# A macaron block on one core: token preparation moved out of the first rounds of each batch, into eight short turns of its second round

## The reference, cut to what matters

```python
x = x + 0.5 * ffn(layernorm(x))     # 8 experts, threshold routing with capacity
x = x + attn(layernorm(x))          # 16 heads of width 16, 4 "nodes" per head
x = x + 0.5 * ffn(layernorm(x))

# attn, per batch b and head h
q, k, v = x @ Wq, x @ Wk, x @ Wv;  probs = softmax(x @ Wr)       # 4 nodes
pos = cumsum(probs over tokens) - probs                            # soft position
cos_w, sin_w = sum over nodes of probs * (cos, sin)(pos * freq), interpolated
q_r, k_r = rotate(q), rotate(k) by cos_w, sin_w
scores = q_r @ k_r.T / sqrt(16) + log(probs @ probs.T + 1e-8)     # causal
out = softmax(scores) @ v;  return out @ Wo
```

## Time and profile before

| | us |
|---|---|
| median of 3 runs | 2910.24 (2907.36 to 2912.67) |
| the profiled execution: its time | 2896.46 |
| its span, first to last instruction | 2894.6 |
| units of the attention (first to last exp) | 536.0 to 2528.7 |
| busy PE / DVE / ACT / POOL | 2448.1 / 1711.7 / 1702.9 / 997.9 |

### The profile page before, as it was taken

How to read it: one execution, slowest core, us unless ns; L and a number is a source line. 1 busy time by engine, 2 the same in 40 slices (tenths; PEclk the granted TensorE clock), 3 DMA queues, 4 the chain that set the end, 5 groups by cost and what they waited for, 6 DMA issues and landing times. The chain is left out here.

```text
span 2894.6 us, 104325 instructions
## 1 busy us (share of the span) xinstructions
PE 2448.1 (85%) x45990; PEld 1896.7 (66%) x45990; DVE 1711.7 (59%) x3627; ACT 1702.9 (59%) x2174; POOL 997.9 (34%) x1497
## 2 busy tenths in 40 slices
PE   7298444587899999899999989999999999973885
PEld 4165222466788887778888777888877888841553
DVE  7732278788576567866566786666676111167431
ACT  6222123456677777667777766777776777662221
POOL 1188700334222224423222442222244222110787
PEclk9699776799999999999999999999999999986997
DMA  6555401221212112212111221211122111162565
GB/s 233 160 103 101 78 18 30 60 53 47 60 57 56 48 46 79 66 49 59 55 53 52 79 66 53 58 53 53 54 74 69 44 47 49 42 204 72 105 102 74
DMA packets 185109, 207.28 MB, mean 72 GB/s; under 512 B 35984, under 2 KB 151712, under 8 KB 184480
## 3 DMA queue, kind: packets, MB, share of 16 engines
q1 hardware_dynamic: 158880, 165.60, 19.3%
q0 software_dynamic: 24576, 34.10, 7.6%
q10 hardware_dynamic: 1152, 0.26, 0.0%
HBM read 131.68 MB, written 76.02 MB: 72 GB/s over the span
## 5 line engine op out<-in xcount | busy, mean ns | idle before, releaser
L1697 PEld LDWEIGHTS at_mix<-at_val,at_ew 128*64 128x64 f32 x34816 | 1223.7, 138 | 241.3 <-issue 36.0
L1281 ACT ACTIVATE at_ew<-at_ring 128x1024 f32<-128x1024 f32 (+1 forms) x1280 | 1124.7, 898 | 364.4 <-PE at_ring L1679 358.2
L1697 PE MATMUL at_mix<-at_val,at_ew 128*64 128x68 f32 x34816 | 1263.0, 224 | 44.7 <-DVE at_mixed L1543 28.7
L1679 PE MATMUL at_ring<-at_qT,at_kT 98*64 98x512 bf16 (+3 forms) x5120 | 698.9, 353 | 57.9 <-ACT at_ew L1281 35.8
L1202 POOL TENSOR_SCALAR_AFFINE_SELECT at_ew<-at_ew 128x256 f32<-128x256 f32 x512 | 294.3, 579 | 1074.2 <-ACT at_ew L1281 1073.5
L1543 DVE TENSOR_TENSOR at_mixed<-at_mix,at_prob 128x272 f32<-128x272 f32 x256 | 112.3, 439 | 440.4 <-PE at_mix L1697 439.1
L1679 PEld LDWEIGHTS at_ring<-at_qT,at_kT 98*64 98x64 bf16 x5120 | 228.5, 112 | 111.4 <-ACT at_ew L1281 47.6
L1224 POOL TENSOR_TENSOR at_val<-at_vo,at_val 128x256 f32<-128x256 f32 x384 | 267.4, 717 | 7.5
L344 POOL DMA_INDIRECT out_dram<-ffn_xn,ffn_idx_all x128 | 210.0, 1641 | 43.4 <-issue 35.0
L334 POOL DMA_INDIRECT ffn_xn<-table,ffn_idx_all x128 | 126.2, 986 | 278.4 <-DMA ffn_idx_all<-ffn_idx_hi 240.3
L1762 PE MATMUL at_side<-at_w_all,at_turned 128*64 128x512 f32 (+1 forms) x1024 | 197.8, 531 | 13.8 <-DVE at_bounded L1536 5.2
(11 more groups left out here) (243 smaller groups left out, 2727.1 us busy)
## 6 DMA issues: line engine op xcount, KB each, us to landing
table<-ffn_xn SPq DMA_DIRECT2D x32, 512.0 KB, 6.3
q_parts<-at_parts SPq DMA_DIRECT2D x64, 192.0 KB, 2.5
k_parts<-at_parts SPq DMA_DIRECT2D x64, 192.0 KB, 3.0
at_qT<-q_parts SPq DMA_DIRECT2D x128, 96.0 KB
at_kT<-k_parts SPq DMA_DIRECT2D x64, 192.0 KB
ffn_front<-in_L_attn_x_dram SPq DMA_DIRECT2D x16, 512.0 KB, 5.3
ffn_w_in<-in_L_ffn_w_dram SPq DMA_DIRECT2D x32, 256.0 KB, 3.6
at_xin<-out_dram SPq DMA_DIRECT2D x32, 256.0 KB, 6.0
```

Source lines behind the costliest of these rows:

```text
L1281: act.activation(ew[u % NE_BUF][:, a:b], ring[u % 2][:, a:b], ACT.Exp).then_inc(s["exp_ready"], 1)
L1679: lastm = pe.matmul(ring[u % 2][h:h + HALF, at:at + (CH - t) * P], kT[q][:, kc + j * P + h:kc + j * P + h + HALF], qT[q][:, qc + t * P:qc ...
L1697: m = pe.matmul(mix[block_of[u] % 2][h:h + HALF, t * K * VW:(t + 1) * K * VW], ew[u % NE_BUF][:, col + h:col + h + HALF], val[q][:, tile0 ...
```

## The change

1. **Turns follow the rounds.** Round 0 keeps four SHORT turns. The second round of each batch has eight MID turns of 28 units. The first rounds of batches 1 to 3 are BARE: no step of preparation or output in them. Each pair is still ready in time, since the eight MID turns of a batch prepare the eight pairs of the next. In the last second round nothing is left to prepare, and all eight turns carry a `post`.
2. **New places.** MID: PE (1, 3, 6, 8, 10, 12, 14, 17, 21, 23); ACT copy_turned 3, copy_v_logits 5, copy_outputs 8, softmax_exp 7, square 10, high_part 14, middle_part 16, low_part 20, trig 18, copy_qk 25, next_rsqrt 17. PE's weighting without reserve is at places 16 to 22. SHORT on ACT: trig 17 (was 16), low_part 19 (18), next_rsqrt 16 (20).
3. **Small steps on DVE.** Rotation, positions, angles, products and sums are cut in more steps, each at a place of its own; in MID turns products and sums go in quarters.
4. **Rotated tiles in transpose mode.** turn_rotated does eight transposes of 128x128 instead of sixteen matmul calls.

```diff
-    turns, at = [], 0
-    while at < U:
-        m = len(turns)
-        turns.append((at, SHORT if m < N_SHORT else LONG))
-        at += turns[-1][1]
+    rounds = [first_unit[v] for v in range(V) if v == 0 or visits[v][1] != visits[v - 1][1]] + [U]
+    turns, m = [], 0
+    for r in range(len(rounds) - 1):
+        size = rounds[r + 1] - rounds[r]
+        count, kind = (N_SHORT, SHORT) if r == 0 else (N_MID, MID) if r % 2 else (1, BARE)
+        for n in range(count):
+            turns.append((rounds[r] + n * (size // count), size // count, kind, None if kind == BARE else m))
+            m += kind != BARE
...
+    STORE_AT = (20, 21, None)
...
-        BURST = 26
+        BURST, BURST_END = 16, 22
...
-                    if at == (10 if short else 14) and new is not None:
+                    if at == (10, 12, None)[kind] and new is not None:
                         add_up(new)
...
-                SHORT_AT = (3, 6, None, 8, 9, 12, 15, 18, 16, 23, 20)
-                LONG_AT = (4, 6, 10, 8, 16, 18, 20, 23, BURST + 2, BURST + 4, BURST + 3)
+                SHORT_AT = (3, 6, None, 8, 9, 12, 15, 19, 17, 23, 16)
+                MID_AT = (3, 5, 8, 7, 10, 14, 16, 20, 18, 25, 17)
...
-                SHORT_AT = (0, 1, 6, 8, None, 10, 12, 13, 14, 18, 19, 20, 21, 23)
-                LONG_AT = (1, 2, 5, 8, 10, 14, 17, 20, 22, 30, 32, 25, 34, 33)
...
+                AT = {"weights": (1, 1), "rotate": (2, 2), "rotate_2": (2, 3), "join": (3, 4), "squares": (14, 16), "bound": (20, 22),
+                      "residual": (None, 9), "shift": (6, 5), "softmax": (8, 8), "positions": (10, 11), "whole": (10, 11),
+                      "first_angles": (11, 12), "count_turns": (12, 13), "angles": (13, 13), "absolute": (13, 14),
+                      "statistics": (15, 15), "normalise": (23, 18)}
+                PRODUCTS_AT = ({18: 0, 21: 2}, {19: 0, 21: 1, 23: 2, 25: 3})
+                SUMS_AT = ({19: 0, 22: 2}, {20: 0, 22: 1, 24: 2, 26: 3})
...
                             for n in range(4):
                                 for g in range(G):
-                                    for h in range(0, P, HALF):
-                                        at = (g * 4 + n) * P + h
-                                        lastm = pe.matmul(side[h:h + HALF, n * GP + g * P:n * GP + (g + 1) * P],
-                                                          qkr[:, at:at + HALF], ident[:, :],
-                                                          start=(n % 2 == 0 and g == 0), stop=False, skip_group_check=True)
+                                    at = (g * 4 + n) * P
+                                    lastm = pe.matmul(side[:, n * GP + g * P:n * GP + (g + 1) * P], qkr[:, at:at + P], ident[:, :],
+                                                      is_transpose=True, start=(n % 2 == 0 and g == 0), stop=False, skip_group_check=True)
...
-                LONG_AT = (1, 3, 7, 9, 13, 15, 17, 20, 24, BURST)
+                MID_AT = (1, 3, 6, 8, 10, 12, 14, 17, 21, 23)
...
-                    if not short and (at == 0 or at >= BURST):
+                    if kind == MID and BURST <= at <= BURST_END:
                         weigh_until(u)
```

More of the change, by code:

```diff
@@ L825, in build_attention @@
     LEAD = 5
-    SHORT, LONG = 24, 40
-    N_SHORT = 4
+    SHORT, MID, BARE = 0, 1, 2
+    N_SHORT, N_MID = 4, 8
     TAIL = TP - 4
@@ L926, in fin_of @@
     def fin_of(m):
-        return LEAD + m - 1 if LEAD + m - 1 < TP else None
+        return LEAD + m - 1 if m is not None and LEAD + m - 1 < TP else None
     with ExitStack() as ctx:
@@ L1060, in schedule @@
             first_visit()
-            for m, (start, size) in enumerate(turns):
-                for at in range(min(size, U - start)):
-                    unit(start + at, at, size == SHORT, new_of(m), fin_of(m), posts.get(m))
+            for start, size, kind, m in turns:
+                for at in range(size):
+                    unit(start + at, at, kind, new_of(m), fin_of(m), posts.get(m))
             last_projections()
@@ L1132, in first_visit, with unit @@
                     load_heads(1)
-                def unit(u, at, short, new, fin, post):
+                def unit(u, at, kind, new, fin, post):
                     if u + 2 in first_unit and u + 2 < U:
@@ L1641, in unit @@
[L1641 to L1650, removed]
+                    if kind == BARE:
+                        return
@@ new lines, in unit @@
+                    step = [name for name in AT if AT[name][kind] == at]
+                    per = 2 if kind == SHORT else 1
+                    if fin is not None:
+                        if "weights" in step:
+                            turn_weights()
+                        if "rotate" in step:
+                            rotate(fin, 0)
+                        if "rotate_2" in step:
+                            rotate(fin, 1)
+                        if "join" in step:
+                            join_halves()
+                        if "squares" in step:
+                            largest_squares(fin)
+                        if "bound" in step:
+                            bound(fin)
@@ new lines, in unit @@
+                    if post is not None and "residual" in step:
+                        add_residual(post, 0, 1)
+                    if new is not None:
+                        if "shift" in step:
+                            shift_logits(new)
+                        if "softmax" in step:
+                            node_softmax(new)
+                        if "positions" in step:
+                            positions(new)
+                        if "whole" in step:
+                            whole_positions()
+                        if "first_angles" in step:
+                            first_angles(new)
+                        if "count_turns" in step:
+                            count_turns()
+                        if "angles" in step:
+                            angles()
+                        if "absolute" in step:
+                            absolute_angles(new)
+                        if at in SUMS_AT[kind] and at in PRODUCTS_AT[kind]:
+                            node_sums(SUMS_AT[kind][at], per)
+                            node_products(new, PRODUCTS_AT[kind][at], per)
+                        elif at in PRODUCTS_AT[kind]:
+                            node_products(new, PRODUCTS_AT[kind][at], per)
+                        elif at in SUMS_AT[kind]:
+                            node_sums(SUMS_AT[kind][at], per)
@@ L1652, in last_projections @@
+                    if more:
+                        if "statistics" in step:
+                            statistics(new + 1)
+                        if "normalise" in step:
+                            normalise(new + 1)
                 def last_projections():
```

88 lines of the change are left out of this document (41 added, 47 removed).

## The result

| | before | after |
|---|---|---|
| median, us | 2910.61 | 3090.10 (3088.8 to 3097.3) |
| ratio, 95% interval | | 1.0623 (1.0604 to 1.0642) |
| the profiled execution: time / span | 2896.46 / 2894.6 | 3088.8 / 3086.8 |
| units of the attention | 1993 | 2176 |

The change makes the kernel 6.2% slower. The forecast was 3070 us, 5.5% slower. The windows of the changed kernel by round: length, busy PE, PEld, DVE, ACT, POOL, granted clock, DMA share, GB/s.

The account below looks back on a forecast made before the run. PE was taken to bound the second rounds, without idle. From 2896.5: - 50.7 - 18 + 214 + 3 + 12 = 3056.8, plus 13.8 to the median gives 3070 us, 5.5% slower; range 2945 to 3125, the forecast's own 3020 to 3110.

Parts of the forecast that it names:

- To which sort of turn MID belongs: MID turns in second rounds: PE waits 9.3 us each, near SHORT's 9.5, where LONG has none; 214 us over 23 turns.
- First rounds, laid bare: First rounds of batches 1 to 3: PE's waits for late mixing and masks all go, 50.7 us saved.
- Transposes: turn_rotated on PE: eight transposes take 1.3 us instead of 1.91 per pair, 18 us saved in all.
- ACT's copies: MID turns: PE waits for ACT's steps two places behind its own, 3.1 us per turn together.
- The sine step: ACT's sines in MID turns: 4.2 us of PE wait plus 0.6 at low_part, 4.8 per turn; bounds 1.6 and 4.8.
- The 0.6 for low_part: MID turns, place 20: low_part finds no reserve after the sines, so PE waits 0.6 us more.
- The clock: MID turns: lower clock level after the sines' wait costs PE 1.4 us per turn; bounds 0 and 2.5.
- PE's busy time: Sign in second rounds: a MID turn with post near 56 us, 46 to 47 of them PE busy.
- Round 0: SHORT turns: next_rsqrt ahead of the sines waits for statistics, 3 us per turn, 12 in all; bounds 0 and 20.
- The rival by which MID behaves like LONG: Second rounds: added waits are hidden, 2854 us, or 2880 with half the bare rounds' gain; chance 0.13.
- The head loads: Rival in bare rounds: loads late by 2 us in each of 24 visits, 48 us lost, 3118 us; 0.07 with another rival.

Follow-up runs that it names:

- e4: Changed kernel with e2's next_rsqrt places, plus ACT's MID copies three places behind PE's steps instead of two; ratio 1.0107 to the kernel before.
- e5: Changed kernel with MID places laid out as LONG's, sines under PE's project_qk, SHORT places as before; ratio 0.9736 to the kernel before.
- e6: e5 with five of ACT's MID steps one place earlier, two places behind PE instead of three; ratio 0.9927 to the kernel before.
- e1: Kernel before with only the rotated tiles turned in transpose mode; 2878.12 against 2896.14 us, ratio 0.9939.
- e2: Changed kernel with next_rsqrt behind the sines on ACT (MID 19, SHORT 20, other ACT SHORT places as before); ratio 1.0369 to the kernel before.
- e3: Changed kernel with sine and cosine of pairs 9 to 31 replaced by two scaled copies, no table loads; 2978.96 us, ratio 1.0286 to the kernel before.
- e7: e5 with the sine step alone moved from place 26 to 21 of ACT's MID turn; ratio 1.0170 to the kernel before.

## Why the prediction was right, point by point

- **To which sort of turn MID belongs.** Right, and shown: by the waits in the trace of after, by e4 (three places for two), e5 and e6.
- **First rounds, laid bare.** Forecast was that all 50.7 us of idle go. They went down to 2.0 to 2.4 us per round, 6.6 in all, and in e5 to 10. The reason given was right: in the first round of batch 1 PE waited 10.3 us for DVE's mixing and 4.3 us for POOL's masks, and in the changed kernel it waits for neither. e5 against e1 gives 59 us, more than the forecast, but only 41 of them are idle time; the 18 us of busy time, which went together with the lower level of the clock, were not forecast.
- **Transposes.** Forecast 18 us, measured 18 (e1), with some luck: the saving was taken as 0.6 us per pair and it is 0.8 by the records' lengths, and a part of it did not reach the time. The Trainium skill's 275 ns for one ("TensorE: Matmul & The Clock Gate", Part 4) agrees with the trace, where a record lasts 279 ns on average. Paid one behind the other they would have made the kernel slower, and that is not what this case shows: eight take 1.09 us.
- **ACT's copies.** Forecast 0.4, 0.1, 0.2, 1.0, 0.6, 0.8. In the turn shown: 0.26, none over 0.12 for the next two, 0.88, 0.65, 0.81. Their sum is 2.7 instead of 3.1 us of idle.
- **The sine step.** Forecast 4.2 us of wait, of which next_rsqrt's standing for the statistics was named; measured 0.88 + 3.58 = 4.5, and ACT's standing 1.89. e2 shows the part of the statistics, e3 that of the tables, e7 that the step alone does it. The last pair has no statistics behind it to wait for, and there the changed kernel's own wait is 2.33 us, as in e2. The 0.6 for low_part did not come in the changed kernel; in e2, where the long wait is shorter, 0.50 stands there.
- **The clock.** Forecast 1.4 us per turn, and right. A turn with a post that has 0.97 is 1.2 us longer than one that has 1.00, and one that has 0.94 is 2.1 to 2.5 us longer. Behind the wait of 3.58 us, which 22 turns have, the clock stayed up in 4, fell for the shorter time in 12 and for the longer in 6, which makes about 1.3 us on average.
- **PE's busy time.** This is the term that the sum did not have. A turn of 57.2 us has 49.95 us of PE busy time, and even one with the clock at 1.00 has 48.56, where e5 has 47.00 for the same work; the prediction said 46 to 47 of 56. So 1.4 us are the lower level, and 1.6 us are there at full clock: this is the step that fell short, since a stop costs PE more than its idle time. The sum per turn was 9.3 us instead of 57.2 - 47.0 = 10.2.
- **Round 0.** Forecast + 12 besides the transposes, found + 16 with them. Against e1's 199.8 us, which has the transposes too, it is + 18, so this term was a third too small. ACT stands 6.04 us for the statistics in a SHORT turn (PE 5.66 us, then 2.23), and e2 gives back 14 us by ACT's list alone. The wait for the head load at the end of the round went from 6.46 to 5.48 us.
- **The whole.** The forecast is 20 us under the measured median, but a part of that is chance. Its sum was reckoned between profiled executions and comes to + 160 us; between the two profiled executions the difference is 192, so that 32 us are missing. The three dense rounds take 1347 us where e5 takes 1114, 233 more against 216 forecast (17 of the 32). Round 0 adds 6, the stretch behind the attention 9, and the transposes gave 4 us less over the units than was put down for them; the bare rounds gave 9 more, which takes away from it. The rest is in the last round, the lead and rounding. The medians are closer, because the profiled execution of the kernel before was 14 us under its median and the changed kernel's only 1.
- **Not forecast.** Behind the last exp the changed kernel takes 374.0 us, the one before 365.2. The code there is the same. Over the other kernels this stretch is 363.5 (e2), 366.6 (e3), 366.7 (e1), 367.9 (e6), 368.1 (e4), 372.8 (e7) and 372.9 (e5), in no relation to how long the attention took. What sets it is open, and so is whether these 9 of the 192 us are the change's at all.

The rival by which MID behaves like LONG fell: its point of decision was 2.3 us of wait per turn, and the turn has 7.3 of idle. e5 shows that it was a matter of places and not of density: LONG's behaviour can be had in 28 units. The head loads do not bound the bare rounds: PE waits for them 1.6 to 2.0 us in a whole round, where the rival had 2 us per visit.

## What to carry to other kernels

Where one engine is busy all the time and takes its input from a second one in order, a step on the second engine that waits for the first costs the step plus the next input less the work that the first has in hand; one more unit of distance makes it free, and whether it is free can be worked out from three durations before anything is built. The longest step of the helping engine belongs beside the longest step of the bound engine, and nothing that waits for a third engine belongs ahead of it. Spreading a fixed amount of helper work more thinly or densely matters less than these two: e5 and the changed kernel do the same work in the same number of units, 8.4% apart, while bare rounds and dense turns against LONG turns (e5 against e1) are worth 2.0%. And a slower clock costs only what no later wait takes in: a turn at 0.97 is 1.2 us longer than one at 1.00 in the changed kernel, 0.4 in e2, where two later waits of 0.5 and 0.3 us go in exchange, and no longer in e4.

## What the runs showed of the hardware that I had not expected

- A wait of PE costs busy time as well, at full clock. e6 has 0.7 us more of it per turn than e5 for four stops (47.75 against 47.00), and e2 and e3 have 1.6 and 1.7 us more for nine and eight, about 0.2 us per stop. The rows have most of this: a group of 32 weightings is 1.11 us long, but the group behind it starts 0.95 us after it did (1302.48 and 1303.43 in e5), and where PE stops behind it, the 0.16 us are no longer covered. No run takes it apart further.
- Long waits of PE were mostly followed by a stretch at the lower level of the clock, but the length of the wait alone does not decide. Behind 3.44 us (e7) it came in 22 of 23 turns, behind 3.58 us (changed) in 18 of 22, behind 2.33 us (e2) in 12 of 23, behind 2.29 us (e4) in 14 of 23, and turns with the same waits at the same places went either way. The Trainium skill, "TensorE: Matmul & The Clock Gate", section "Why this matters for your kernels", asks to avoid long idle gaps of the engine between bursts of matmuls; the trace agrees for most of the long ones, and here shorter waits brought the lower level too. Over the units the lower level lasts 145 us in the changed kernel, 68 in the one before and 33 in e5.
